# Silu in one instruction, b1 on sets of 32 partitions, mean terms by VectorE: a feed-forward block with cross-attention

## The chip, the cores and the metric

The kernel runs on one core of one Trainium2 chip. The metric is the device time of one execution in microseconds, the median of several runs.

## The reference

The input x has 32 tiles of 128 rows and 512 columns; ctx has the same shape, and a mask says for each of the 32 batches which of its 128 context rows count. With LN(x) = (x - mean) / sqrt(var + 1e-5):

```
scores = LN(x) @ ctx^T / sqrt(512), masked;  x = x + softmax(scores) @ ctx
y  = LN(x)
h  = silu(bitlinear(y, w1, b1))            # 512 -> 2048
h  = gelu(h, exact)
h  = layer_norm(h) * ln_g + ln_b           # over 2048
out = x + bitlinear(h, w2, b2)             # 2048 -> 512

bitlinear(x, w, b): xq = round(rms(x) * 127 / absmax) ...   # per row, 8 bits
                    wq = round(w / mean|w|) clipped to -1, 0, 1, times mean|w|
                    xq @ wq^T + b
```

## The kernel before

Everything is written by hand: five engine programs, each a list of calls in one fixed order, with semaphores between them. A tile t is one batch (128 rows). Each call below handles one tile, or two where it says (t, 2).

For a tile, TensorE sums the context's columns for two tiles at once (`column_sums`, L576 to 585, into the PSUM tensor `ba`). ScalarE multiplies these sums by the row means of x (`mean_term`, L1170, one instruction of 128 columns per tile), so that TensorE can work on x before it is normalised. `scores` (L564) adds a mask term (one row of `maskb` against ones, L569) and four fp32 products, in `ba` again, so the scores of a pair wait until its mean terms have been read out (`s_corr`). VectorE's `softmax` (L1902) centres them, ScalarE's `exp_scores` (L1164) takes exp, TensorE turns the probabilities and makes the readout (L587, L594), VectorE adds it to x (`add_readout`, L1916), GpSimd centres and rounds to q1 (L1555, L1569), and SyncE turns q1 by a transposing DMA.

The first product (`first_product`, L613) has two halves h. Each fills 1024 columns of `z_ps[h]` with eight matmuls of 512 columns (L623) and adds b1 with two more (L628), whose left side is `brows`, the turned factors of the tile, and whose right side is `rows1`, b1 in three bf16 parts crossed with three parts of the factor: 9 rows of 2048 columns. The factors are split by GpSimd (`split_factors`, L1576), turned by TensorE (L600), and copied by VectorE (`copy_factors`, L1950). ScalarE's `silu(t, h)` (L1192) reads one half, so that TensorE can refill the other half's PSUM as soon as one silu is done. Then come `gelu` (L1201) with its sum, the mean by GpSimd (`gelu_mean`, L1595), `variance` (L1207) on ScalarE, `rstd` on GpSimd (L1600), VectorE's three instructions of 2048 columns `gained`, `normed` and `norm_absmax` (L1961, L1973, L1982), ScalarE's `square_l` (L1218), GpSimd's rounding to q2 (L1612), a transposing DMA, the second product (`second_product`, L632) and `output` on VectorE (L2011).

Silu, gelu and exp need different function tables on ScalarE; where the order changes from one to another, the compiler puts an ACT_TABLE_LOAD. Squares, copies and scaling need none of their own. `warm` (L538) multiplies an idle tile, to keep TensorE working.

SyncE issues all DMAs in one written order. In the first 60 us it brings w1 and w2 (4 MB each, in quarters), gain and beta (1 MB each, broadcast to 128 partitions), and the first tiles of x, its transpose xT, ctx and its transpose ctxT (256 KB each). The weights are summed, scaled and rounded on three engines before the first product. The last tiles' rounding is split in halves between VectorE and ScalarE.

## Time and profile before

| | |
|---|---|
| median of 3 runs | 419.42 us (418.55 to 420.19) |
| the profiled execution | 418.72 us, span 416.8 us |
| ScalarE (ACT) busy | 381.7 us |
| TensorE (PE) busy | 380.0 us |
| VectorE (DVE) busy | 366.0 us |
| GpSimd (POOL) busy | 270.1 us |

Busy time is the union of an engine's instructions; a mean duration counts each alone, so neighbours that overlap add up to more than their share. The span is that of one execution in the hardware profile. PEld is TensorE's weight load, which overlaps its matmuls. PEclk, the clock granted to TensorE, is 1.00 at full speed.

### The profile page before, as it was taken

What the parts mean: (1) busy time and instruction counts of PE and PEld (TensorE: products, weight loads), DVE (VectorE), ACT (ScalarE), POOL (GpSimd) and SP (SyncE); (2) the same over time, 40 slices, a digit from 0 to 9 for tenths busy, and PEclk for the clock granted to TensorE, in tenths of its full rate; (3) what the DMA queues carried; (4) which work ended last, traced back from release to release, by engine and by line L of the source; (5) the groups of instructions that cost most, each with busy time, mean ns of one, the idle gap of its engine ahead of it and who ended that gap; (6) DMA issues with size and microseconds to landing.
All of it is one profiled execution on the core that took longest, in us unless ns stands there. A gap on an engine that the chain in (4) does not pass through costs nothing.

```text
span 416.8 us, 6814 instructions
## 1 busy us (share of the span) xinstructions
PE 380.0 (91%) x1878; PEld 202.8 (49%) x1878; DVE 366.0 (88%) x571; ACT 381.7 (92%) x517; POOL 270.1 (65%) x373
## 2 busy tenths in 40 slices
PE   3889888788999999999999999999999987899896
PEld 2576444444555544544555455554545432444342
DVE  5378589999999989999999999989998689999992
ACT  2597999999999999999999999999999999999960
POOL 6368588764787738664875569485368855477930
PEclk9999998999999999999999999999999996999999
DMA  7999991556665695658568765694754423083585
GB/s 290 412 366 320 393 289 39 176 131 143 196 172 119 177 225 158 157 164 197 150 168 239 201 171 147 201 218 102 187 133 94 91 63 63 2 201 102 90 213 128
DMA packets 108853, 73.87 MB, mean 177 GB/s; under 512 B 87048, under 2 KB 87056, under 8 KB 107536
## 3 DMA queue, kind: packets, MB, share of 16 engines
q1 hardware_dynamic: 108816, 73.43, 64.7%
q8 instruction: 16, 0.26, 0.3%
q14 instruction: 21, 0.17, 0.1%
HBM read 44.05 MB, written 8.39 MB: 126 GB/s over the span
## 4 chain that ended last, share of the span: by engine, by line
issue 23%; PE 22%; ACT 21%; DVE 19%; POOL 9%; DMA 4%; DVEq 0%; SPq 0%; POOLq 0%; ACTq 0%
ACT junk_v L1210 6%; DVE hid L1979 6%; PE z L623 6%; PE acc L648 5%; DVE hid L1970 5%; ACT hid L1205 4%; ACT hid L1199 4%; PE ba L573 3%; DMA xT<-in_xT_dram 3%; POOL hid L1616 3%; PE ba L584 2%; DVE am L1984 2%; PE z L628 2%; POOL rstd L1605 2%; PE bb L598 2%
## 5 line engine op out<-in xcount | busy, mean ns | idle before, releaser
L623 PE MATMUL z<-w1q,q1T 128*128 128x512 f16 x512 | 122.6, 383 | 3.9 <-ACT hid L1199 3.9
L648 PE MATMUL acc<-w2q,q2T 128*128 128x512 f16 x512 | 117.4, 379 | 1.2 <-DMA q2T<-hid 1.2
L1979 DVE SCALAR_TENSOR_TENSOR hid<-hid,rstd,beta 128x2048 f32<-128x2048 f32 x32 | 76.7, 2400 | 5.9 <-POOL rstd L1605 5.5
L623 PEld LDWEIGHTS z<-w1q,q1T 128*128 128x128 f16 x512 | 49.4, 98 | 65.1 <-ACT hid L1199 10.7
L1970 DVE SCALAR_TENSOR_TENSOR hid<-hid,nmu,gain 128x2048 f32<-128x2048 f32 x32 | 79.3, 2477 | 0.4 <-POOL nmu L1597 0.3
L648 PEld LDWEIGHTS acc<-w2q,q2T 128*128 128x128 f16 x512 | 49.8, 98 | 59.0 <-DMA q2T<-hid 2.0
L1984 DVE TENSOR_REDUCE am<-hid 128x1 f32<-128x2049 f32 x32 | 72.5, 2269 | 0.1
L1199 ACT ACTIVATE hid<-z,fac 128x1024 f32<-128x1024 f32 x64 | 70.7, 1118 | 0.8 <-PE z L628 0.5
L1221 ACT ACTIVATE junk_l<-hid 128x2050 bf16<-128x2050 f32 x32 | 61.1, 1910 | 3.7 <-DVE hid L1979 3.4
L1616 POOL TENSOR_SCALAR hid<-hid,kq 128x2048 f16<-128x2048 f32 x30 | 60.9, 2031 | 4.6 <-DVE kq L1991 3.0
L1210 ACT ACTIVATE junk_v<-hid,gsum 128x2048 bf16<-128x2048 f32 x32 | 63.7, 1990 | 0.1
L1205 ACT ACTIVATE hid<-hid 128x2048 f32<-128x2048 f32 x32 | 60.9, 1904 | 0.2
L628 PE MATMUL z<-rows,brows 128*128 128x512 bf16 x128 | 38.5, 383 | 1.4 <-DVE brows L1959 1.4
L584 PE MATMUL ba<-ctxT,neg 128*128 128x256 f32 x128 | 32.4, 398 | 6.5 <-DMA ctxT<-in_ctxT_dram 6.3
L573 PE MATMUL ba<-ctxT,xT 128*128 128x128 f32 x256 | 36.6, 287 | 1.9 <-DMA xT<-in_xT_dram 1.9
L1574 POOL TENSOR_SCALAR q<-xc,kq 128x512 f16<-128x512 f32 x32 | 33.8, 1056 | 4.9 <-DVE kq L1932 3.0
L598 PE MATMUL bb<-ctx,probT 128*128 128x512 f32 x64 | 34.2, 617 | 0.5 <-ACT probT L1181 0.5
L573 PEld LDWEIGHTS ba<-ctxT,xT 128*128 128x128 f32 x256 | 31.8, 195 | 4.7 <-issue 3.1
L1567 POOL TENSOR_TENSOR rho<-sq,c_neghalf 128x2 f32<-128x2 f32 (+1 forms) x17 | 14.7, 867 | 27.0 <-ACT junk_x L1189 27.0
L584 PEld LDWEIGHTS ba<-ctxT,neg 128*128 128x128 f32 x128 | 24.8, 199 | 12.7 <-issue 8.0
L1603 POOL TENSOR_SCALAR ve<-vsum 128x2 f32<-128x2 f32 (+1 forms) x18 | 9.9, 548 | 31.0 <-ACT junk_v L1210 30.6
L1920 DVE SCALAR_TENSOR_TENSOR xs<-bb,rsum,xs 128x512 f32<-128x512 f32 x32 | 23.8, 743 | 6.0 <-PE bb L598 5.9
(105 smaller groups left out, 569.4 us busy)
## 6 DMA issues: line engine op xcount, KB each, us to landing
ctxT<-in_ctxT_dram SPq DMA_DIRECT2D x32, 256.0 KB, 3.6
xs<-in_x_dram SPq DMA_DIRECT2D x32, 256.0 KB, 3.5
xT<-in_xT_dram SPq DMA_DIRECT2D x32, 256.0 KB, 3.7
ctx<-in_ctx_dram SPq DMA_DIRECT2D x32, 256.0 KB, 3.5
out_dram<-xs SPq DMA_DIRECT2D x32, 256.0 KB, 2.9
hid<-in_w1T_dram SPq DMA_DIRECT2D x4, 1024.0 KB, 9.4
hid<-in_w2T_dram SPq DMA_DIRECT2D x4, 1024.0 KB, 7.4
gain<-in_g_dram SPq DMA_DIRECT2D x1, 1024.0 KB, 10.5
```

The costliest lines, as they stand in the source:

```text
L573: mm = pe.matmul(score_ps, xT[:, t % XT, c, :], ctxT[:, t % CT, c, :], start=False, stop=(c == DC - 1))
L584: mm = pe.matmul(csum_ps, neg[:, :], ctxT[:, t % CT:t % CT + 2, c, :], start=(c == 0), stop=(c == DC - 1))
L623: pe.matmul(z_ps[h][:, c * CH:(c + 1) * CH], q1T[:, t % 4, k, :], w1q[:, k, f0:f0 + CH], start=(k == 0), stop=False)
L648: mm = pe.matmul(a, q2T[:, t % 2, c, :], w2q[:, c, :], start=False, stop=(c == FC - 1))
L1199: act.activation(hid[:, t % HR, half(h)], z_ps[h][:, :], ACT.Silu, scale=fac[:, t, 0:1]).then_inc(s_silu[h], 1)
L1205: act.activation(hh, hh, ACT.Gelu, accum_out=gsum[:, t:t + 1]).then_inc(s_gelu, 1)
L1210: act.activation(junk_v[:, :], hid[:, t % HR, 0:FF], ACT.Square, bias=gsum[:, t:t + 1], scale=-float(FF), accum_out=vsum[:, t:t + 1]).then ...
L1221: act.activation(junk_l[:, :], hid[:, row_of(t), 0:FF + 2], ACT.Square, scale=ROOT2, accum_out=ysum[:, t:t + 1]).then_inc(s_sq, 1)
L1616: pool.tensor_scalar(q2_of(t), hid[:, row_of(t), 0:FF], kq2[:, t:t + 1], UNIT, ALU.mult, ALU.mult).then_inc(s_q2, 1)
L1970: dve.scalar_tensor_tensor(out=hid[:, row_of(t), 0:FF], in0=hid[:, t % HR, 0:FF], scalar=nmu[:, t:t + 1], in1=gain[:, :], op0=ALU.add, op1 ...
L1979: dve.scalar_tensor_tensor(out=hh, in0=hh, scalar=rstd[:, t:t + 1], in1=beta[:, :], op0=ALU.mult, op1=ALU.add).then_inc(s_l, 1)
L1984: dve.tensor_reduce(am2[:, t:t + 1], hid[:, row_of(t), 0:FF + 1], AX_X, ALU.max, apply_absolute_value=True).then_inc(s_am2, 1)
```

## The change

- `z_ps` is one PSUM tensor of 2048 columns. `silu(t)` is one instruction over all of it; the first product of the next tile waits for the whole of it, and the signal that z is ready comes once per tile.
- The factors are repeated for four sets (bands) of 32 partitions. `rows1` is now 128 x 512: band c holds the rows for columns 512c to 512c+511. The four products with b1 come together at the end of the second half, each with 32 partitions of `brows` and of `rows1`, into four PSUM banks. `invert_factors` writes four copies, `split_factors` splits all of them, `copy_factors` copies 128 partitions instead of 18.
- The mean terms of two tiles are one VectorE instruction (`mean_terms`), and ScalarE has none. `gelu_mean` goes from GpSimd to VectorE.
- The mask is loaded by one DMA and turned into a bias once; `scores` picks its row by a column of the identity.
- `turn_factors` no longer waits for the output of an earlier tile by itself; that wait now stands in TensorE's order in front of the call.
- All five orders are written anew. Among other things, SyncE asks for x tiles 9 to 12 and beta ahead of gain (17.6 MB asked for up to and with gain before, 19.1 now) and for ctxT 8 and 9 later (16.6, now 20.1 MB); GpSimd rounds both of its w1 parts one behind the other; ScalarE's order has 51 changes of function table where it had 48; warm blocks go from 20 to 34, of which 29 stand ahead of the second product of tile 5; on VectorE 11 instead of 9 `x_stats` stand ahead of `gained(0)`, and `gelu_mean` of tiles 21, 22 and 23 ahead of `gained(21)`.

```diff
@@ first product, TensorE
-                wait(pe, s_silu[h], t)
-                pe.wait_ge(s_q1T[t % 4], landed(t, 4))
+                if h == 0:
+                    wait(pe, s_silu, t)
+                    pe.wait_ge(s_q1T[t % 4], landed(t, 4))
                 for k in range(DC):
-                    for c in range(2):
-                        f0 = h * HALF + c * CH
-                        pe.matmul(z_ps[h][:, c * CH:(c + 1) * CH], q1T[:, t % 4, k, :], w1q[:, k, f0:f0 + CH],
+                    for c in range(2 * h, 2 * h + 2):
+                        pe.matmul(z_ps[:, c * CH:(c + 1) * CH], q1T[:, t % 4, k, :], w1q[:, k, c * CH:(c + 1) * CH],
                                   start=(k == 0), stop=False)
-                pe.wait_ge(s_brow, t + 1)
-                for c in range(2):
-                    f0 = h * HALF + c * CH
-                    mm = pe.matmul(z_ps[h][:, c * CH:(c + 1) * CH], brows[:, t % 4, :], rows1[:, f0:f0 + CH],
-                                   start=False, stop=True)
-                mm.then_inc(s_z[h], 1)
+                if h == 1:
+
+                    pe.wait_ge(s_brow, t + 1)
+                    for c in range(BANDS):
+                        band = slice(c * BAND, (c + 1) * BAND)
+                        mm = pe.matmul(z_ps[:, c * CH:(c + 1) * CH], brows[band, t % 4, :], rows1[band, :],
+                                       start=False, stop=True)
+                    mm.then_inc(s_z, 1)
@@ silu, ScalarE
-                act.wait_ge(s_z[h], t + 1)
-                act.activation(hid[:, t % HR, half(h)], z_ps[h][:, :], ACT.Silu, scale=fac[:, t, 0:1]).then_inc(s_silu[h], 1)
+                act.wait_ge(s_z, t + 1)
+                act.activation(hid[:, t % HR, 0:FF], z_ps[:, :], ACT.Silu, scale=fac[:, t, 0:1]).then_inc(s_silu, 1)
@@ mean terms: ScalarE (gone) and VectorE (new)
-            def mean_term(t):
-
-                act.wait_ge(s_csp, t // 2 + 1)
-                act.wait_ge(s_mv1, t + 1)
-                wait(act, s_centred, t - CR + 1)
-                act.activation(corr[:, t % CR, :], csum_ps[:, t % 2 * P:(t % 2 + 1) * P], ACT.Identity,
-                               scale=mv1[:, t, 0:1]).then_inc(s_corr, 1)
+            def mean_terms(t):
+
+                dve.wait_ge(s_csp, t // 2 + 1)
+                dve.wait_ge(s_mv1, t + 2)
+                wait(dve, s_centred, t - CR + 2)
+                dve.tensor_tensor(corr[:, t % CR:t % CR + 2, :], csum_ps.rearrange("p (a m) -> p a m", a=2),
+                                  mv1[:, t:t + 2, 0:1].to_broadcast((P, 2, P)), ALU.mult).then_inc(s_corr, 2)
@@ mean of gelu: GpSimd (gone) and VectorE (new)
-            def gelu_mean(t):
-                pool.wait_ge(s_gelu, t + 1)
-                pool.tensor_scalar(nmu[:, t:t + 1], gsum[:, t:t + 1], -1.0 / FF, 0.0,
-                                   ALU.mult, ALU.add).then_inc(s_nmu, 1)
+            def gelu_mean(t):
+                dve.wait_ge(s_gelu, t + 1)
+                dve.tensor_scalar(nmu[:, t:t + 1], gsum[:, t:t + 1], -1.0 / FF, None, ALU.mult).then_inc(s_nmu, 1)
@@ factors, VectorE
-                dve.reciprocal(inv[:, of, :], fac[:, of, :]).then_inc(s_inv, n)
+                dve.reciprocal(inv[:, of, :, :], fac[:, of, :].unsqueeze(2).to_broadcast((P, n, BANDS, 2))).then_inc(s_inv, n)
@@ mask term, TensorE
-                pe.matmul(score_ps, ones_b[:, :], maskb[:, t // G % 2, t % G, :], start=True, stop=False)
+                pe.matmul(score_ps, ident_b[:, t:t + 1].to_broadcast((P, P)), maskb[:, :], start=True, stop=False)
```

## Rows read from the trace of the kernel before

**Rows 1.** The page: the span, and busy us (share of the span) xinstructions of each engine.

```profile
span 416.8 us, 6814 instructions
PE 380.0 (91%) x1878; PEld 202.8 (49%) x1878; DVE 366.0 (88%) x571; ACT 381.7 (92%) x517; POOL 270.1 (65%) x373
```

**Rows 2.** Busy us of each engine in four stretches; then clock, DMA share, GB/s.

```profile
0.00:40.00 40.00, 30.43 (x188) 22.60 (x189) 25.62 (x65) 23.04 (x46) 24.79 (x58) 1.00 0.95 344
40.00:57.30 17.30, 15.32 (x77) 8.35 (x75) 9.98 (x32) 17.19 (x27) 11.05 (x21) 1.00 1.08 365
57.30:400.00 342.70, 321.60 (x1560) 166.47 (x1558) 321.76 (x463) 338.32 (x443) 232.13 (x287) 0.99 0.60 149
400.00:416.80 16.80, 12.61 (x59) 5.37 (x57) 8.67 (x15) 3.15 (x3) 2.09 (x9) 0.98 0.62 164
```

**Rows 3.** Groups by line and form, ScalarE: busy us, mean ns | idle before.

```profile
L1199 ACT ACTIVATE hid<-z,fac 128x1024 f32<-128x1024 f32 x64 | 70.7, 1118 | 0.8 <-PE z L628 0.5
L1205 ACT ACTIVATE hid<-hid 128x2048 f32<-128x2048 f32 x32 | 60.9, 1904 | 0.2
L1199 ACT ACT_TABLE_LOAD x17 | 21.8, 1283 | 1.0 <-PE z L628 0.7
...
L1175 ACT ACTIVATE corr<-ba,mv 128x128 f32<-128x128 f32 x32 | 11.1, 365 | 4.1 <-PE ba L584 4.1
...
L1143 ACT ACTIVATE w2q<-hid 128x1024 f16<-128x1024 f32 x4 | 4.2, 1048 | 0.0
```

**Rows 4.** ScalarE's timeline from 180.8 to 185.7 us: start, us, what.

```profile
180.81 0.37 ACT L1175 ACTIVATE corr<-ba,mv 128x128 f32<-128x128 f32 x1
181.06 1.12 ACT L1199 ACTIVATE hid<-z,fac 128x1024 f32<-128x1024 f32 x1
182.06 0.29 ACT L1181 ACTIVATE probT<-bb 128x128 f32<-128x128 f32 x1
...
183.74 0.24 ACT L1189 ACTIVATION_READ_ACCUMULATOR junk_x<-xc 128x1 f32 x1
184.00 1.28 ACT L1167 ACT_TABLE_LOAD   x1
185.29 0.40 ACT L1167 ACTIVATE prob<-score,nbias 128x129 f32<-128x129 f32 x1
```

**Rows 5.** Groups by line and form, VectorE.

```profile
L1920 DVE SCALAR_TENSOR_TENSOR xs<-bb,rsum,xs 128x512 f32<-128x512 f32 x32 | 23.8, 743 | 6.0 <-PE bb L598 5.9
...
L1898 DVE BATCH_NORM_STATS2 st<-xs 128x6 f32<-128x512 f32 x32 | 22.1, 692 | 1.2 <-DMA xs<-in_x_dram 1.2
...
L1908 DVE CUSTOM_DVE_ANT_0 score<-corr,ba,nrs 128x128 f32<-128x128 f32 x32 | 11.0, 344 | 16.6 <-PE ba L573 14.1 <-POOL nrs L1553 2.1 <-issue 0.2
...
L1876 DVE TENSOR_SCALAR wfac<-wmean 128x1 f32<-128x1 f32 x2 | 0.3, 134 | 0.0
```

**Rows 6.** Groups by line and form, TensorE: the products with b1.

```profile
L628 PE MATMUL z<-rows,brows 128*128 128x512 bf16 x128 | 38.5, 383 | 1.4 <-DVE brows L1959 1.4
```

**Rows 7.** TensorE's timeline at 181 us: start, us, what.

```profile
181.25 0.59 PE L628 MATMUL z<-rows,brows 128*128 128x512 bf16 x2
181.68 0.22 PE L569 MATMUL ba<-maskb,ones_b 128*128 128x128 bf16 x1
```

**Rows 8.** The timeline of SyncE's queue: the issue of gain's load.

```profile
43.60 0.52 SPq L281 DMA_DIRECT2D gain<-in_g_dram  x1
```

**Rows 9.** The page's DMA issues: KB each, us from issue to landing.

```profile
gain<-in_g_dram SPq DMA_DIRECT2D x1, 1024.0 KB, 10.5
```

**Rows 10.** VectorE's timeline: its first instruction with gain.

```profile
57.27 2.35 DVE L1970 SCALAR_TENSOR_TENSOR hid<-hid,nmu,gain 128x2048 f32<-128x2048 f32 x1
```

**Rows 11.** TensorE's timeline: the column sums of tiles 8 and 9.

```profile
55.57 1.99 PE L584 MATMUL ba<-ctxT,neg 128*128 128x256 f32 x8 [0.21 <-DVE nbias L1908]
```

**Rows 12.** Waits of the whole span: engine line <- releaser: us in total, times, longest.

```profile
DVE hid L1979 <- POOL rstd L1605: 5.5, 8, 1.3
...
PEld ba L569 <- ACT corr L1175: 5.3, 5, 2.2
```

2046 lines of the change are left out of this document (974 added, 1072 removed).

## The prediction

> **What bounds the kernel now.** I read the page's busy times first. Three engines are nearly full over the 416.8 us of the profiled execution: ScalarE 381.7, TensorE 380.0, VectorE 366.0; GpSimd has 270.1 [rows 1]. An average over a start, a middle and a tail hides the limit, so I cut the span where VectorE begins its first 2048-column instruction (57.3 us) and where its last ones end (400). In the 342.7 us between, ScalarE is busy 338.32, which leaves it 4.4 us idle; TensorE has 321.60 (21.1 idle) and VectorE 321.76 (20.9 idle) [rows 2]. So the middle, four fifths of the time, goes at ScalarE's pace, about 11.7 us a tile. The start (0 to 57.3) is another matter: the DMA engines are full (shares 0.95 and 1.08) while 8 MB of weights and the first tiles come in [rows 2], and VectorE idles. In the last 16.8 us ScalarE is nearly done and VectorE works 8.67 us; what is left is the chain of the last tile. The reader should see that a microsecond taken from ScalarE is worth a microsecond only until the next engine is full, and that VectorE stands only 16.6 us behind in the middle.
>
> **ScalarE, what goes.** Silu was two instructions of 1024 columns, mean 1118 ns [rows 3]. One of 2048 is not in the trace. The step from 1024 to 2048 columns is taken from two forms of other functions, 1048 and 1904 ns [rows 3]: 0.856 us. So one whole silu is 1.118 + 0.856 = 1.974 us against 2.236, a gain of 0.26. But neighbours overlap: the silu that begins at 181.06 and lasts 1.12 is followed at 182.06 [rows 4], so of the fixed part only about 0.15 is time on the engine. With some 30 tiles in the middle that is 4.5 to 7.8 us, and I take 5, since the step from start to start is what fills an engine. The mean terms leave ScalarE: 365 ns each by duration [rows 3], 0.25 from start to start (180.81 to 181.06) [rows 4]; 24 of them lie in the middle, 6.0 to 8.8 us, and I take 7. The copy of b1 (9 rows of 2048 columns) becomes 128 rows of 512; it lies in the start, where the weights' arrival decides, so I give it nothing; it is worth about a microsecond if that cover is gone.
>
> **ScalarE, what is added.** A table load comes wherever the function changes between exp, silu and gelu; each is 1283 ns [rows 3]. Counting the changes in the written orders gives 48 before and 51 after, so 3 more: 3.85 us. The trace shows such a load between 184.00 and 185.28, directly behind the instruction that ended at 183.98 and directly ahead of the exp at 185.29 [rows 4]: nothing is lost around it. The Trainium skill, "ScalarE: Activation LUTs", section "What ACT_TABLE_LOAD costs", puts about 1380 ns of drain on top of the load's 1283 for every switch. By that rule the three added loads would be an estimated 8.0 us rather than 3.85, and the forecast 4 us later; the rows just read speak against it. Sum for ScalarE's middle: 338.3 - 5 - 7 + 3.9 = 330.2 us (bounds 325.6 and 331.7).
>
> **VectorE, what is added.** Mean terms: 16 instructions over 2 x 128 columns of PSUM, about 12 in the middle. Nearest rows are the softmax step with 128 columns from PSUM, 344 ns, and the readout's addition with 512, 743 ns [rows 5]; on the line between them 256 columns cost 0.48. Less an overlap of the same kind as on ScalarE, 0.4 to 0.48: 4.8 to 5.8 us; the lower end could be 12 x 0.28, but a tensor operand that reads two tiles at once gives no reason for less. The mean of gelu moves over from GpSimd, one value per partition: 134 ns by the nearest row [rows 5], and less where it overlaps: 30 x 0.08 to 30 x 0.13, 2.4 to 4. The reciprocal over 16 instead of 4 values and the copy of factor rows from 128 instead of 18 partitions cost nothing that shows (lanes work side by side). Two more x_stats stand ahead of the first gained than before (11 against 9 in the two orders): -2 x about 0.8, from 692 ns [rows 5]. Sum: 321.8 + 5.3 + 3.0 - 1.6 = 328.5 us (bounds 327.4 and 330).
>
> So after the change ScalarE (330) and VectorE (328.5) carry the same load in the middle. That is the core of the forecast: about 8 us leave the bounding engine, and the next one rises by 7 to meet it.
>
> **TensorE.** The four products with b1 last 383 ns each [rows 6], but two are through in 0.59 us and the next instruction begins 0.43 behind the first (181.25, 181.68) [rows 7]: a step of 0.216, so 0.86 us of a tile's time. If the four run at once on four sets of 32 partitions, 0.22 is left, a saving of 0.64 x 30 = 19 us; if they run one behind the other, nothing. TensorE has 21 us idle in the middle already [rows 2] and waits for others, so I give either case nothing in the sum. With z in one piece, the next tile's first product must wait for the whole silu (1.97) where it waited for half; the written order puts readouts, scores or second products there, and ScalarE has two squares of 2048 and two of 512 columns between most pairs of silus, some 5 us by the 1904 ns of such a length [rows 3], more than a first product (16 x 0.216 = 3.5) needs. So nothing, and up to 1 us a pair if the filler is late. Of the 34 warm blocks 29 stand in the first part, ahead of the second product of tile 5, where TensorE waits anyway.
>
> **GpSimd** loses 32 means and 7 mask instructions and gets four times wider splits of the factors, from 4 to 16 values and from 12 to 48; it is busy 65% and pays nothing.
>
> **The start.** I add up the bytes in the written order of SyncE's queue, up to and with gain: 17.6 MB before, 19.1 after (more x tiles, and beta ahead of gain). Gain was issued at 43.60 [rows 8] and landed 10.5 us later [rows 9], at 54.1, and the first gained began at 57.27 [rows 10], 3.2 later. At the 365 GB/s of that stretch [rows 2], 1.5 MB more are 4.3 us: landing at 58.4, 1.1 later than the instruction began. w1's columns are rounded earlier by the new GpSimd order, but that can't bring the first gained ahead of its operand. So +1.1 (0 if the queue runs fuller, 3 if SyncE's waits for q1 hold it). Context tiles 8 and 9 move back as well, from 16.6 to 20.1 MB, so to about 61; their column sums began at 55.57 [rows 11] and stand ahead of the first product of tile 3 on TensorE. That is late by up to 3 us, and ScalarE has the squares and gelus of tiles 0 to 2 to cover it; without that cover it is the same 3 us.
>
> **The sum.** VectorE: 58.4 (start) + 328.5 (work) + idle in the middle + 16.8 (tail, left as it is). That is 403.7 + idle. The bounding engine of before idles 4.4 us; VectorE, which had to wait for it, 20.9. With both equally loaded I take 8, above the first, since each now waits for the other: the largest of VectorE's waits for another engine's result, 5.5 us for rstd, comes through GpSimd from ScalarE's variance [rows 12], and gets shorter as ScalarE gets ahead. Span 411.7. The profiled execution ran 418.72 for a span of 416.8, so +1.9: 413.6, against its own 418.72. The median of the runs, 419.42, stands 0.7 above that execution: 414.3 is predicted.
>
> **The rivals.** (A) VectorE has taken ScalarE's place fully and the idle hardly shrinks: idle 12 to 13, which gives 403.7 + 12.5 + 2.6 = 418.8, no change. For it: the new VectorE order puts up to three means of gelu (21, 22, 23) ahead of gained(21), so that VectorE waits for a later gelu than it needs. Against it: ScalarE gains 8 us. (B) The products with b1 don't run side by side, or TensorE pays for each change between whole and banded products. A matmul lasts 383 ns and steps 216 [rows 6, 7], so a change that waits for the last one to end is priced at the difference, 0.17; two such per tile are 10 us in the middle. Serial and with that, TensorE has 321.6 + 10 = 331.6, a third engine at the same load, with idle of about 13: 419. The Trainium skill, "TensorEngine Tiling (Array Packing)", section "Key Properties", says that a change of tiling mode drains the engine; no row of before shows one. With the four at once and that price, TensorE is at 312 and harmless. (C) Slower: the mean terms now queue on VectorE behind its instructions of 2.35 us [rows 10], with the scores waiting for them on TensorE and everything behind these in order. Before, TensorE's weight loads for the scores waited 5.3 us in all for them [rows 12]. TensorE's idle of 21 plus the 19 saved are some 2.7 us per pair of tiles; the wait decides once it is over that. One such instruction in front stays below, two in front (4.7) are 2.0 over, at 15 pairs up to 30 us. With a quarter of the pairs: 414.3 + 8 = 422 to 423. Against it: in the new order a column sum stands at least 3.5 us of other products ahead of its scores. (D) Better: start unchanged, idle 4.4, lower prices: 57.3 + 327.4 + 16.8 + 4.4 + 2.6 = 408.5.
>
> **How the numbers follow.** Forecast (idle 6 to 11) 0.42; D 0.22; A 0.12; B 0.07; C 0.17. Faster by over 0.5% means under 417.3: forecast and D, 0.64. Within 0.5%, about what a measurement here can tell from no change: A and B, 0.19. Slower than 421.5: C, 0.17. The range reaches from 407 (D with silu at its best) to 423 (the near side of C).
>
> **What the next profile would show.** Right: silu x32 at 1.97 us; 51 loads; mean terms 0.4 to 0.5 on VectorE; VectorE busy 373 to 378 and ScalarE 366 to 371; VectorE idle in the middle under 11; first gained at 58 to 59; TensorE busy below 370 and the four band products within 0.6 us. Wrong: scores waiting for the mean terms by more than 10 us in all (C); a gained longer than the 2.35 us of before; band products stepping at 216 ns (B); a start that is later by more than 3 us.

## The result, and the profile after

The changed kernel takes 425.44 us (median of 4 runs, 422.52 to 426.14) against 418.99 for the kernel before in the same series: ratio 1.013, interval 1.0106 to 1.0154. It is slower, by 1.3%. The prediction was 414.3 us, with a range of 407 to 423, and faster as the likeliest sign. The profiled execution took 422.52 us for a span of 420.7, 3.9 more than the 416.8 of [rows 1]. It is the shortest of the four; the other three took 425.25 to 426.14 us, spans of 423.5 to 424.3. So what follows accounts for these 3.9 us, and some 2.5 of the 6.45 by which the medians differ are not in the trace.

The page of the changed kernel, the span and the engines' busy time:

```profile
span 420.7 us, 6729 instructions
PE 375.8 (89%) x1943; PEld 199.8 (47%) x1962; DVE 366.7 (87%) x619; ACT 373.4 (89%) x456; POOL 281.1 (67%) x333
```

Against [rows 1] ScalarE lost 8.3 us of work, TensorE 4.2, VectorE gained 0.7 and GpSimd 11.0. No engine got fuller in share except GpSimd, and the time still rose, so the time has gone into waits. To see where, I cut both traces at two events of ScalarE that exist in both: its first silu, and the gelu of tile 26. First the kernel before (columns as in rows 2):

```profile
0.00:39.44 39.44, 29.87 (x186) 22.34 (x187) 25.06 (x64) 22.48 (x46) 24.23 (x58) 1.00 0.95 343
39.44:343.02 303.58, 287.33 (x1398) 151.91 (x1396) 277.31 (x440) 300.33 (x413) 203.90 (x263) 0.99 0.65 171
343.02:416.80 73.78, 62.77 (x296) 28.55 (x296) 63.66 (x68) 58.89 (x60) 41.93 (x54) 0.95 0.49 113
```

and the kernel after:

```profile
0.00:44.90 44.90, 38.01 (x225) 26.54 (x226) 24.66 (x64) 19.39 (x38) 21.17 (x58) 0.92 1.00 349
44.90:343.23 298.33, 278.71 (x1440) 147.00 (x1453) 278.00 (x483) 293.10 (x363) 218.18 (x232) 1.00 0.64 165
343.23:420.70 77.47, 59.12 (x279) 26.25 (x283) 64.06 (x74) 60.90 (x56) 41.76 (x44) 0.96 0.49 116
```

Three stretches, three answers. The middle is 5.25 us shorter, and ScalarE's own work in it 7.2 us shorter; this is what the change was costed for. The first silu comes 5.5 us later. From gelu(26) to the end it takes 3.7 us longer. The sum is +3.9, the whole difference of the spans. With the old start and the old end the new middle would have given a span of 411.55. That this is close to the forecast's 411.7 is chance: the forecast had the start 1.1 later and its own middle, cut at other places, 6.2 shorter.

The operations themselves, groups by line and form of the kernel after (ScalarE, VectorE, TensorE):

```profile
L1120 ACT ACTIVATE hid<-z,fac 128x2048 f32<-128x2048 f32 x32 | 62.8, 1962 | 0.7 <-PE z L622 0.5
L1120 ACT ACT_TABLE_LOAD x19 | 24.4, 1283 | 2.6 <-PE z L622 2.3
L1125 ACT ACT_TABLE_LOAD x18 | 23.1, 1283 | 0.3
L1096 ACT ACT_TABLE_LOAD x14 | 18.0, 1283 | 0.9 <-PEq L2366 0.7
...
L1825 DVE SCALAR_TENSOR_TENSOR hid<-hid,nmu,gain 128x2048 f32<-128x2048 f32 x32 | 75.8, 2375 | 5.9 <-ACT junk_v L1130 5.8
L1761 DVE TENSOR_TENSOR corr<-ba,mv 128x256 f32<-128x256 f32 x16 | 6.6, 412 | 0.5 <-DVE mv L1744 0.4
...
L615 PE MATMUL z<-w1q,q1T 128*128 128x512 f16 x512 | 120.3, 385 | 14.4 <-ACT hid L1120 14.4
L622 PE MATMUL z<-rows,brows 32*128 32x512 bf16 x128 | 12.6, 385 | 0.0
```

The whole silu lasts 1.962 us (costed at 1.974), the mean terms of two tiles 0.412 (costed at 0.40 to 0.48), and there are 51 table loads, as costed. The products with b1 fell from 38.5 us of TensorE's time [rows 6] to 12.6. What they cost now is seen in TensorE's timeline (start, us, what):

```profile
50.48 0.40 PE L622 MATMUL z<-rows,brows 32*128 32x512 bf16 x4
50.80 0.33 PE L585 MATMUL bb<-ident,prob 128*128 128x128 f32 x1
```

Four products are through in 0.40 us, and the next instruction begins 0.32 behind the first, where four steps of 0.216 would have been 0.86 [rows 7]. They do run at once. TensorE as a whole did not fall below 370 us as forecast (375.8), since 14 warm blocks were added. Beside it stands a row that the forecast had priced at nothing, and up to 1 us a pair: TensorE's first product (L615) now waits 14.4 us for silu, 3.9 before.

VectorE, on whose load the predicted sum was built, from its first instruction with gain to the last instructions (the cut lies as far behind the last normed as in rows 2):

```profile
60.95:402.80 341.85, 309.98 (x1573) 158.89 (x1589) 320.58 (x503) 334.82 (x397) 245.54 (x250) 0.99 0.59 144
```

Of 341.85 us VectorE is busy 320.58 and idle 21.3. Before it was busy 321.76 and idle 20.9 [rows 2]. In the same stretch ScalarE is busy 334.82 and idle 7.0: it is still the engine with the least idle time. What makes up VectorE's idle time has changed. The wait for rstd fell from 5.5 to 4.0 us, but `gained`, which may only write over the tile when ScalarE's `variance` has read it, now waits 5.8 us for that (the row of L1825 above); before, `gained` waited 0.4 us in all.

### The profile page after: what moved, and what is told of

The parts are those of the page before. It is cut to its first block, busy times and chain, and to the rows that moved or that the text cites. A ratio compares the mean times of both kernels' runs of the same rounds, so it can differ in the third digit from the quotient of the medians.

```text
span 420.7 us, 6729 instructions
## 1 busy us (share of the span) xinstructions
PE 375.8 (89%) x1943; PEld 199.8 (47%) x1962; DVE 366.7 (87%) x619; ACT 373.4 (89%) x456; POOL 281.1 (67%) x333
## 4 chain that ended last, share of the span: by engine, by line
ACT 36%; issue 22%; PE 21%; DVE 14%; DMA 4%; SPq 1%; POOL 1%; ACTq 0%; DVEq 0%; POOLq 0%
ACT hid L1120 8%; PE z L615 7%; ACT junk_v L1130 6%; ACT hid L1125 6%; PE acc L642 6%; ACT junk_l L1141 4%; DVE hid L1825 4%; ACT L1125 3%; ACT L1120 3%; PE ba L566 3%; DVE hid L1834 2%; DMA xs<-in_x_dram 2%; DVE am L1839 2%; ACT L1096 2%; PE bb L591 2%
## 5 line engine op out<-in xcount | busy, mean ns | idle before, releaser
L615 PE MATMUL z<-w1q,q1T 128*128 128x512 f16 x512 | 120.3, 385 | 14.4 <-ACT hid L1120 14.4
L615 PEld LDWEIGHTS z<-w1q,q1T 128*128 128x128 f16 x512 | 49.4, 99 | 75.9 <-ACT hid L1120 19.9
L1825 DVE SCALAR_TENSOR_TENSOR hid<-hid,nmu,gain 128x2048 f32<-128x2048 f32 x32 | 75.8, 2375 | 5.9 <-ACT junk_v L1130 5.8
L1499 POOL TENSOR_SCALAR hid<-hid,kq 128x2048 f16<-128x2048 f32 x30 | 65.1, 2173 | 10.5 <-ACT junk_l L1141 5.6
L1120 ACT ACTIVATE hid<-z,fac 128x2048 f32<-128x2048 f32 x32 | 62.8, 1962 | 0.7 <-PE z L622 0.5
L1448 POOL TENSOR_SCALAR xc<-xs,sum 128x512 f32<-128x512 f32 x32 | 33.8, 1055 | 11.9 <-DVE xs L1772 11.4
L1486 POOL TENSOR_SCALAR ve<-vsum 128x2 f32<-128x2 f32 (+1 forms) x18 | 17.6, 980 | 30.1 <-ACT junk_v L1130 29.8
L1461 POOL TENSOR_SCALAR q<-xc,kq 128x512 f16<-128x512 f32 x32 | 28.6, 896 | 9.6 <-DVE kq L1784 8.4
L534 PE MATMUL z<-idle 128*128 128x256 bf16 x204 | 27.6, 285 | 1.6 <-POOL idle L1384 1.1
L1869 DVE SCALAR_TENSOR_TENSOR xs<-acc,fac,xs 128x512 f32<-128x512 f32 x32 | 23.5, 738 | 6.3 <-PE acc L642 6.1
L1742 DVE BATCH_NORM_STATS2 st<-xs 128x6 f32<-128x512 f32 x32 | 21.6, 676 | 6.7 <-DMA xs<-in_x_dram 6.7
```

The lines of the kernel that those rows point to most:

```text
L615: pe.matmul(z_ps[:, c * CH:(c + 1) * CH], q1T[:, t % 4, k, :], w1q[:, k, c * CH:(c + 1) * CH], start=(k == 0), stop=False)
L1120: act.activation(hid[:, t % HR, 0:FF], z_ps[:, :], ACT.Silu, scale=fac[:, t, 0:1]).then_inc(s_silu, 1)
L1499: pool.tensor_scalar(q2_of(t), hid[:, row_of(t), 0:FF], kq2[:, t:t + 1], UNIT, ALU.mult, ALU.mult).then_inc(s_q2, 1)
L1825: dve.scalar_tensor_tensor(out=hid[:, row_of(t), 0:FF], in0=hid[:, t % HR, 0:FF], scalar=nmu[:, t:t + 1], in1=gain[:, :], op0=ALU.add, op1 ...
```

## The experiments

A run is named here by its kernel; "before" and "after" are the two kernels of the case. The table gives, for the profiled execution of each, four times read from ScalarE's timeline and the span, and beside them the ratio of the timed runs to before. The times are of one execution each, and executions of one kernel differ by up to 6 us (p6_nosilu: 442.71 to 448.65), so small differences in these columns prove nothing by themselves.

| kernel | silu(0) | gelu(2) | gelu(26) | gelu(31) | span | ratio (interval) |
|---|---|---|---|---|---|---|
| before | 39.44 | 69.99 | 343.02 | 392.44 | 416.8 | 1 |
| after | 44.90 | 74.78 | 343.23 | 394.50 | 420.7 | 1.013 (1.0106 to 1.0154) |
| p1_silu | 43.77 | 80.01 | 397.92 | 451.60 | 476.0 | 1.1397 (1.1358 to 1.1435) |
| p4_ops | 44.40 | 77.90 | 393.07 | 446.24 | 471.0 | 1.1282 (1.1248 to 1.1316) |
| p3_mean | 44.94 | 74.71 | 367.63 | 417.04 | 441.4 | 1.054 (1.0502 to 1.0578) |
| p6_nosilu | 42.43 | 72.28 | 370.63 | 421.65 | 446.8 | 1.0651 (1.0589 to 1.0713) |
| p7_mean_placed | 39.81 | 69.60 | 346.23 | 395.67 | 420.0 | 1.0092 (1.0065 to 1.0119) |
| a1_halves | 42.75 | 72.94 | 344.65 | 397.19 | 424.7 | 1.017 (1.0134 to 1.0205) |
| e1_warm | 42.42 | 74.04 | 342.50 | 393.78 | 420.1 | 1.0111 (1.0059 to 1.0162) |
| e5_warm_moved | 44.73 | 74.43 | 342.94 | 394.21 | 420.4 | 1.0127 (1.0068 to 1.0186) |
| e2_warm_stats | 42.27 | 76.75 | 346.05 | 398.53 | 425.9 | 1.0165 (1.0114 to 1.0216) |
| h1_oldstart | 40.26 | 76.34 | 345.62 | 398.18 | 427.3 | 1.019 (1.0164 to 1.0216) |
| h3_oldstart_sp | 41.00 | 72.39 | 340.86 | 393.45 | 422.4 | 1.0076 (1.0042 to 1.0109) |
| e3_tail | 42.12 | 74.90 | 343.37 | 396.91 | 427.1 | 1.0236 (1.019 to 1.0282) |
| e6_end | 43.59 | 74.71 | 343.24 | 395.63 | 424.2 | 1.0144 (1.0119 to 1.0169) |
| e8_end_warm | 42.95 | 75.78 | 344.28 | 396.79 | 423.7 | 1.0104 (1.0043 to 1.0165) |
| e9_end2 | 41.81 | 73.14 | 341.63 | 394.15 | 419.8 | 1.0078 (1.0051 to 1.0106) |
| e7_start_end | 41.98 | 75.48 | 343.99 | 396.22 | 421.9 | 1.0081 (1.0053 to 1.0109) |
| h2_oldstart_end | 40.62 | 75.40 | 343.93 | 396.47 | 423.4 | 1.0147 (1.0115 to 1.0178) |
| h4_both | 40.14 | 71.85 | 340.30 | 392.85 | 418.5 | 1.0034 (1.0015 to 1.0053) |

One reading of the table first: from gelu(2) to gelu(26) it takes 273.03 us in before, and 268.4 to 268.6 in after and in ten kernels that share its middle (269.3 in e2_warm_stats and h1_oldstart). So the middle's gain of 3.7 to 4.6 us is there every time.

### What each part costs on the old orders

**p1_silu**: the kernel before, with only z in one piece and silu whole.

```diff
-act.wait_ge(s_z[h], t + 1)
-act.activation(hid[:, t % HR, half(h)], z_ps[h][:, :], ACT.Silu, scale=fac[:, t, 0:1]).then_inc(s_silu[h], 1)
+act.wait_ge(s_z[0], t + 1)
+act.wait_ge(s_z[1], t + 1)
+act.activation(hid[:, t % HR, 0:FF], z_ps[:, :], ACT.Silu, scale=fac[:, t, 0:1]).then_inc(s_silu, 1)
```

> The kernel before, with one part of the change alone: z in one piece, silu in one instruction of 2048 columns in the place of the second half's, all orders as before. Theory S: ScalarE bounds, the saving is 0.15 us a tile, 32 x 0.15 = 4.8 us, less what TensorE's first products lose by waiting for the whole: ratio 0.989 to 0.995. Rival W: on these orders, ScalarE waits for z that comes late because TensorE may not refill before the whole silu is read; each pair loses a microsecond or more, ratio 1.01 to 1.04.

477.58 us. The part that saves ScalarE 3.9 us of work costs 58 us on the old orders. Its waits (engine line <- releaser: us in total, times, longest):

```profile
PE z L623 <- ACT hid L1200: 43.6, 17, 4.7
ACT hid L1200 <- PE z L628: 38.1, 14, 5.2
```

TensorE waits for silu, and then silu for TensorE, in turn: with one z, and the calls in this order, little is left to work on while the other side is busy. In before the same first wait was 3.9 us.

**p4_ops**: every operation of the changed kernel on the orders of before; calls that moved to another engine stand at the nearest place.

```diff
-silu(24, 0)
-mean_term(30)
-mean_term(31)
-silu(24, 1)
+silu(24)
...
 x_stats(25)
+mean_terms(24)
...
+gelu_mean(24)
 gained(24)
```

> All the operations of the changed kernel (whole silu, b1's four products on sets of 32 partitions, mean terms of two tiles and gelu's mean on VectorE, mask in one) on the orders of the kernel before, the moved calls put in at the nearest place. Theory O (the new orders lose): with 48 table loads, the old start and the old end, it runs 6 to 8 us below the changed kernel, ratio 0.995 to 1.0. Rival Q (the operations themselves lose): mean terms behind VectorE's long instructions hold TensorE, and the ratio is 1.013 or more on whatever order.

472.87 us, 5 less than p1_silu. So of the changed kernel's two sides, the operations lose 54 us on the old orders and the new orders win 47 of them back. The orders aren't a side matter: without them the new operations are ruinous.

**p3_mean** and **p7_mean_placed**: before, with the mean terms alone moved to VectorE. They differ only in where some of the 16 instructions stand: close behind the pair's statistics in p3_mean, and in p7_mean_placed where, in the trace of before, the pair's column sums had just ended. One of the moves, from p3_mean to p7_mean_placed:

```diff
 x_stats(25)
-mean_terms(24)
 norm_absmax(15)
...
 normed(16)
+mean_terms(24)
 x_stats(26)
```

> The kernel before with one part alone: mean terms of two tiles by one VectorE instruction, each placed in VectorE's old order between the pair's statistics and its first softmax and never between two 2048-column instructions; silu stays in halves. Theory M (this part pays alone, since ScalarE sets the pace): ScalarE busy 381.7 less 32 times 0.3 = about 371, time 412 to 416, ratio 0.985 to 0.993. Theory Q (the terms queue behind VectorE's 2.35 us instructions and scores wait for them, the prediction's rival C): ScalarE busy falls the same, but TensorE's wait on the mean terms grows by over 10 us in all, ratio 1.00 to 1.02.

442.18 us: the first form costs 23 us. TensorE's wait for the terms did not grow as theory Q had it; VectorE was the one that stood, waiting for column sums that TensorE's order had not reached, with all that is queued behind it. VectorE's and ScalarE's timelines (start, us, what, and the idle time before it):

```profile
252.14 0.42 DVE L1912 TENSOR_TENSOR corr<-ba,mv 128x256 f32<-128x256 f32 x1 [6.22 <-PE ba L584]
252.48 2.28 DVE L1987 TENSOR_REDUCE am<-hid 128x1 f32<-128x2049 f32 x1
...
263.02 1.91 ACT L1213 ACTIVATE junk_l<-hid 128x2050 bf16<-128x2050 f32 x1 [6.54 <-DVE hid L1982]
```

6.2 us idle on VectorE, 10 us later 6.5 us idle on ScalarE.

> The kernel before with the mean terms on VectorE alone, as in the run that took 442.2 us, but each of the 16 instructions placed where, in the trace of before, the pair's column sums had just left TensorE (that run placed them up to 6.2 us too early, and VectorE stood still in its order behind them). Theory P (the place is the price): the waits of 6.2 and 5.4 us go, ScalarE's wait for VectorE's normed tile falls from 14.7 us to under 5, and ScalarE keeps its 11 us: 410 to 416 us, ratio 0.98 to 0.993. Rival (these small steps on VectorE are late wherever they stand, since 2.35 us instructions lie ahead of them, and the start loses the same 5 us): 420 to 430 us, ratio over 1.003.

422.79 us: the place was worth 19 us, as theory P said. But P's second half fell. ScalarE lost the work (in the middle 294.93 us busy against 300.33) and the middle took 306.42 us against 303.58. It idles 11.5 us there instead of 3.3, the largest share for VectorE's normed tiles (5.0 us over the run). ScalarE's work fell by 7.0 us over the whole run (381.7 to 374.7), 0.22 a tile and not the 11 us of the mean terms' durations; put in small pieces on the next engine, it gave nothing on the old orders. silu(0) is 0.4 us later than in before (39.81), so mean terms on VectorE need not delay the start.

**p6_nosilu**: all operations except the one-piece z, on the old orders, mean terms placed as in p3_mean.

```diff
+if h == 0:
+    for c in range(2):
+        band = slice(c * BAND, (c + 1) * BAND)
+        mm = pe.matmul(z_ps[:, c * CH:(c + 1) * CH], brows[band, t % 4, :], rows1[band, :], start=False, stop=True)
+    mm.then_inc(s_za, 1)
```

> Every operation of the changed kernel except silu in one piece, on the orders of before: mean terms and the small sum on VectorE, b1's products on 32-partition bands (two at once behind each half), the mask as one table; z is released and made ready per half as before. Beside the same with silu whole (472.9 us) it differs only in the one-piece z. Theory H (the one-piece z is the whole loss of the old orders): within 1% of the run with the mean terms alone, ratio 0.98 to 1.00, TensorE's wait for silu back to 3 to 6 us. Rival (bands, mask or the small sum on VectorE cost something by themselves): over 1.01.

447.41 us, 1% over p3_mean, and 25 us under p4_ops, which has the one-piece z besides. So the one-piece z costs 25 us with all else equal here (58 when it is added to before alone), and bands, mask and the small sum on VectorE about 5 together, the difference to p3_mean (one comparison, not taken apart further). Why the one-piece z costs twice as much on before alone was not tested.

### Halves on the new orders

**a1_halves**: after, its orders kept, with silu again in two instructions.

```diff
-silu(t)
+silu(t, 0)
+silu(t, 1)
```

TensorE refills columns 0 to 1023 of z behind the first of the two, and for 23 of the tiles the first half is made ready by itself; tile 0 is not among them.

> The changed kernel, its orders kept, with silu again in two instructions of 1024 columns next to each other; TensorE refills the first half of z after the first instruction, and for 23 of the tiles the first half is made ready alone. Theory S (handshake): the new orders still pay for the one-piece z at the start and at the end; ScalarE busy +5 us, but silu(0) starts 0.5 to 1 us earlier and TensorE's 14.4 us wait for silu falls under 6; time 420 to 425, ratio 1.002 to 1.013, equal to or faster than the changed kernel. Theory R (ScalarE's time is all that counts in the middle): +4 to +5 us, ratio 1.022 to 1.025.

426.33 us, 0.9 more than after; the two ratios' intervals overlap. TensorE's wait for silu fell from 14.4 us to 3.0, as S had it, and brought nothing: from gelu(2) to gelu(26) it takes 271.7 us instead of 268.5, and from silu(0) to gelu(26) ScalarE has 297.4 us of work instead of 293.1. So on orders made for it the one-piece z is worth its work in the middle, and the 14.4 us of waiting cost nothing there. silu(0) comes 2.15 us earlier than in after, but not by the halves: it still waited for all four products with b1. TensorE's first product began at 35.69 instead of 37.36, at a full clock. The ratio of 1.017 lies between what S and R gave. Of the end this run says nothing: a first product there waited 4.8 us for the transposing DMA of its q1.

### The start

The first product of tile 0 is on TensorE's timeline, and silu(0) follows it. Before, from the product's beginning to the two products with b1 that make the first half of z ready, and the same in e9_end2, whose start is that of after call for call:

```profile
35.74 1.89 PE L623 MATMUL z<-w1q,q1T 128*128 128x512 f16 x8
37.47 0.59 PE L628 MATMUL z<-rows,brows 128*128 128x512 bf16 x2
```

```profile
34.71 1.89 PE L615 MATMUL z<-w1q,q1T 128*128 128x512 f16 x8
40.02 0.40 PE L622 MATMUL z<-rows,brows 32*128 32x512 bf16 x4
```

| kernel | z of tile 0 | first product | silu(0) | between |
|---|---|---|---|---|
| before | halves | 35.74 | 39.44 | 3.70 |
| h4_both (old start order) | halves | 36.55 | 40.14 | 3.59 |
| p1_silu (old order) | one piece | 36.16 | 43.77 | 7.61 |
| after | one piece | 37.36 | 44.90 | 7.54 |
| e3_tail (start as after) | one piece | 35.10 | 42.12 | 7.02 |
| e6_end (start as after) | one piece | 36.98 | 43.59 | 6.61 |
| e8_end_warm (start as after) | one piece | 36.55 | 42.95 | 6.40 |
| e9_end2 (start as after) | one piece | 34.71 | 41.81 | 7.10 |

With z of tile 0 in halves silu(0) comes 3.6 to 3.7 us behind the first product in all eight kernels that have it so, and with the whole of z to wait for 6.4 to 7.6 us in the other twelve. So the handshake costs 2.7 us or more at the start, in every execution; in e3_tail and e9_end2 the first product even began earlier than before, and silu(0) was still 2.7 and 2.4 us late. The rest of the 5.5 us of after is of its own execution, and differs from one to the next.

In the trace of after TensorE idles 2.19 us in front of the fifth tile's scores, waiting for VectorE's mean terms; and then its granted clock falls. VectorE's and TensorE's timelines:

```profile
29.05 0.69 DVE L1742 BATCH_NORM_STATS2 st<-xs 128x6 f32<-128x512 f32 x1 [1.53 <-DMA xs<-in_x_dram]
29.88 2.33 DVE L1725 TENSOR_SCALAR w1q<-hid,wscale 128x2048 f16<-128x2048 f32 x1
32.27 0.40 DVE L1761 TENSOR_TENSOR corr<-ba,mv 128x256 f32<-128x256 f32 x1
...
32.72 0.23 PE L562 MATMUL ba<-maskb,ident_b 128*128 128x128 bf16 x1 [2.19 <-DVE corr L1761]
32.82 2.03 PE L566 MATMUL ba<-ctxT,xT 128*128 128x128 f32 x8
37.36 3.03 PE L615 MATMUL z<-w1q,q1T 128*128 128x512 f16 x8
```

Read upwards: the scores wait for mean terms, these stand behind a 2.33 us rounding step of w1, and that stands behind the statistics of tile 5, whose x came 1.53 us late. The granted clock of 30 to 40 us is 0.66, between its two levels of 2.4 and 1.2 GHz. The eight products for scores take 2.03 us; the same eight take 1.11 at full clock (57.07 us), and the half first product 3.03 against 1.89. This is rival C's mechanism, with one 2.33 us instruction in front, in one place instead of a quarter of the pairs: from 100 to 340 us the scores waited only 0.2 us for mean terms. The same wait is in e6_end (2.20 us), but in e3_tail and e9_end2, with the same calls up to there, it is 0.25 us, x was not late, and the clock stays 1.00. So this chain is something that an execution can meet, and not the price of the order.

**e1_warm**: idle matmuls in that gap.

```diff
 readout(2)
+warm(34)
+warm(35)
+warm(36)
 pe.wait_ge(s_corr, 6)
 scores(4)
```

> The changed kernel with three warm blocks (18 matmuls of 256 columns on the idle tile, about 2 us) added on TensorE between the readout of tile 2 and the scores of tile 4. Theory Z (TensorE's clock): in the changed kernel TensorE stands idle for 2.2 us ahead of those scores, then the granted clock is at the lower of its two levels from about 32 to 40 us, and the scores (2.0 instead of 1.1 us), the readout (2.1 for 1.0) and the first half of the first product (3.0 for 1.9) take some 3 us more on the way to the first silu. With the gap filled the first silu begins at about 42 instead of 44.9 us and the whole comes 3 us earlier, a ratio to the kernel before near 1.006. Rival Y (the start is hidden): VectorE or the DMAs decide when the pipeline is full, the first silu comes earlier but the end stays, 1.013.

The clock stays 1.00 from 20 to 45 us and silu(0) comes 2.5 us earlier than in the trace of after. That this is the blocks' doing is not shown: e3_tail and e9_end2 have it at 42.12 and 41.81 without them. gelu(2) is 0.7 earlier, and the time 423.88 (1.0111), its interval over that of after. silu(2) waits 1.9 us for a first product that stands behind four more warm blocks.

**e5_warm_moved**: e1_warm without these four.

```diff
-warm(14)
-warm(15)
 readout(5)
-warm(16)
 scores(7)
-warm(17)
 first_product(2, 0)
```

> The changed kernel with three blocks of idle matmuls between the third readout and the fifth tile's scores (they keep the clock up, as in the first experiment), and without the four blocks 14 to 17 that stood ahead of the third tile's first product. In the first experiment silu(2) waited 1.94 us for that product, behind 3.3 us of idle matmuls. Theory N (those blocks took back what the clock gave): gelu(2) starts at 72.0 to 72.8 instead of 74.0, time 421 to 422.5, ratio 1.004 to 1.008. Rival (the pair after it is held by VectorE or a load, or the clock falls again without the blocks): gelu(2) at 74 or later, ratio 1.011 or more.

silu(2) no longer waits for z, but in this execution the clock had already fallen to 0.54 from 15 to 20 us, silu(0) came at 44.73, and the ratio is 1.0127. Undecided on its own: taking idle matmuls out at one place while the clock falls at another.

**e2_warm_stats**: two warm blocks, and the rounding step ahead of tile 5's statistics.

```diff
 readout(2)
+warm(34)
+warm(35)
...
 softmax(3)
-x_stats(5)
 round_w1(1)
+x_stats(5)
```

> The changed kernel with, at the start, two blocks of idle matmuls after the third readout and VectorE's rounding step of w1 ahead of tile 5's statistics, which waited 1.5 us for tile 5's load. Theory N2 (the wait for the load shifts the mean terms of the third pair and with them silu(0)): silu(0) at 41.0 to 42.0 instead of 44.9, and since the blocks 14 to 17 are still there, gelu(2) only at about 73.5 to 74: ratio 1.008 to 1.012. Rival (another input is late): silu(0) at 42.4 or later, no gain on the first experiment.

silu(0) at 42.27, no better than e1_warm, in whose execution x(5) had not been late (0.04 us), so a late x(5) is not what remains. gelu(2) came at 76.75, with a granted clock of 0.89 from 45 to 75 us. A miss: 1.0165.

**h1_oldstart**: each engine works off the order of before up to about 53 us, with silu of tiles 0 and 1 in halves and mean terms placed as in p7_mean_placed; then the rest of the new order, without warm blocks 14 to 17.

```diff
 weight_total(1)
-pe.wait_ge(s_corr, 8)
-scores(6)
-pe.wait_ge(s_wmean[1], 1)
-turn_factors(2)
 pe.wait_ge(s_turn, 6)
 readout(4)
+pe.wait_ge(s_wmean[1], 1)
+turn_factors(2)
+pe.wait_ge(s_corr, 8)
+scores(6)
 turn_factors(3)
 pe.wait_ge(s_silu, 2)
-warm(14)
-warm(15)
 readout(5)
...
```

Shown is the seam in TensorE's order (behind turn_factors(2)); on ScalarE it lies behind gelu(1), on VectorE behind x_stats(8), on GpSimd behind centre_x1(5), and on SyncE behind load_beta. Calls already made are left out of the rest.

> All operations of the changed kernel; each engine first works off the order of before up to about 53 us (ScalarE up to the gelu of tile 1, with mean terms placed as in the run of 422.8 us and silu of tiles 0 and 1 in halves), and then the rest of the new order, with silu in one piece and without the idle blocks 14 to 17. Theory L (what was lost at the start is the new start order with its one-piece z, and the middle of the changed kernel is good by itself): silu(0) at 39.5 to 40.5, gelu(2) at 70 to 71.5 instead of 74.8, span 416 to 418, ratio 0.995 to 1.002. Rival F (what is late at 75 us is VectorE's and GpSimd's backlog, which comes back in another place): gelu(2) earlier, but gelu(8) at 142 or later, ratio 1.008 or more.

silu(0) is 4.6 us earlier than in after, 3.59 us behind a first product that began at 36.67. Then everything waited for one transpose. SyncE's queue and TensorE:

```profile
56.18 1.20 SPq L257 DMA_TRANSPOSE q1T<-q  x1
...
66.08 2.29 PE L621 MATMUL z<-w1q,q1T 128*128 128x512 f16 x5 [5.95 <-DMA q1T<-q]
```

In before tile 3's transpose was issued at 45.41; here the seam had put it behind four x loads and, among others, two ctxT loads that wait for free buffers.

**h3_oldstart_sp**: that one line moved.

```diff
 load_beta()
+transpose_q1(3)
 load_x(10)
...
 load_xT(8)
-transpose_q1(3)
```

> The old start on the new middle once more, with one line moved in SyncE's queue: the transpose of tile 3's q1 stands where it stood in before, right behind the load of beta, instead of behind four x loads, the gain's followers and four ctxT loads. In the first try silu(0) was 4.6 us earlier than in the changed kernel, but tile 3's first product waited 5.95 us for this transpose (issued at 56.2 instead of 45.4) and gelu(2) came at 76.3. Theory L: gelu(2) at 69.5 to 71.5, span 415.5 to 418, ratio 0.994 to 1.002. Rival F (backlog of the other engines): gelu(2) early, gelu(8) at 141.5 or later, ratio 1.006 or more.

gelu(2) 72.39, 4 us earlier than in h1_oldstart, 2.4 earlier than in after, and it keeps this to gelu(26) (340.86 against 343.23). 423.57 us, ratio 1.0076. Theory L is right in kind: something was lost at the start, and what is won back there is kept through the middle. But it is half of the 4.8 us by which gelu(2) was late, and in this execution the end, unchanged, takes 81.5 us from gelu(26) instead of 77.5, more than was won. Old order and halves came together in the h kernels; by the table above silu(0) is earlier by the halves, since the first product is not (37.41).

### The end

Between gelu(26) and the end ScalarE has 2.0 us more to do (60.90 against 58.89): two of the three extra table loads lie there, since the new order goes from silu to gelu and back for each of the last tiles. And VectorE asks for the small sum of tile 31 ahead of the row maximum of tile 30, so it waits for gelu(31), and outputs, scales and TensorE's last products are late in turn.

**e3_tail**: after, with ScalarE's order from silu(28) as in before, two loads fewer.

```diff
 silu(28)
-gelu(28)
 square_l(24)
 square_l(25)
-variance(28)
 silu(29)
+gelu(28)
 gelu(29)
+variance(28)
...
```

> The changed kernel with the end of ScalarE's order (from silu of tile 28 on) laid as in the kernel before: silu 28, silu 29, gelu 28, gelu 29 instead of silu, gelu, silu, gelu; 49 function-table loads instead of 51, two fewer than in the changed kernel, both in the end. Theory T: ScalarE bounds up to the last silu, so the two loads (2 x 1.28 us) are worth 2.6 us and the end is 2 to 3.7 us earlier, ratio 1.004 to 1.008. Rival: VectorE's 2048-column instructions set the last 70 us, the loads are hidden, ratio 1.013.

428.66 us, 4.8 slower than e1_warm of the same series. silu(29) waits 1.8 us for z and silu(30) 3.6. So in this order the two loads fewer are paid for with longer waits for the one z: two silus can't follow each other closely. Theory T fell.

**e6_end**: VectorE's end reordered, three warm blocks left out.

```diff
-warm(31)
-warm(32)
-warm(33)
 second_product(28, 0)
...
-gelu_mean(31)
 norm_absmax(30)
 output(27)
 copy_factors(34)
+gelu_mean(31)
 gained(31)
...
+q2_scale(31, 1)
 output(28)
 out_scale(31, 1)
-q2_scale(31, 1)
```

> The changed kernel with its last 30 us rearranged only: on VectorE the row maximum of tile 30 goes ahead of tile 31's small sum (which waited 0.83 us for tile 31's gelu with the row maximum behind it), tile 31's scale goes ahead of tile 28's output, and TensorE's three blocks of idle matmuls ahead of the last four second products are left out. In the trace of after these products began at 401.63, 4.3 us later than in before, and then ran almost without a gap. Theory E (the order at the end costs over 2 us of the 3.7): span 1.8 to 3 us shorter than 420.7, ratio 1.005 to 1.009. Rival (the end hangs on the two extra table loads and on gelu(31), 2.1 us late): under 1 us, ratio 1.011 or more.

1.0144, a miss. The last products began at 399.33 instead of 401.63, but then TensorE idled 2.26 and 1.48 us, the granted clock fell to 0.50 (410 to 415 us), and eight products took 3.62 us instead of 1.89. It was also slow earlier, where nothing had been changed. The same two stretches of after and of e6_end:

```profile
370.00:375.00 5.00, 3.90 (x20) 1.41 (x19) 4.89 (x7) 4.97 (x6) 3.30 (x6) 0.92 1.11 208
375.00:380.00 5.00, 4.95 (x24) 2.24 (x24) 4.00 (x3) 4.97 (x5) 1.34 (x2) 1.00 0.02 4
```

```profile
370.00:375.00 5.00, 3.53 (x10) 1.08 (x9) 4.89 (x7) 4.97 (x6) 3.31 (x6) 0.50 1.12 208
375.00:380.00 5.00, 4.95 (x25) 2.08 (x25) 4.00 (x3) 3.87 (x5) 1.36 (x2) 0.97 0.02 5
```

At a clock of 0.50 instead of 0.92, tile 30's first product is 1.1 us late and ScalarE idles 1.1 us (4.97 busy against 3.87). gelu(30) comes 42.55 us behind gelu(26) in after, e1_warm and e5_warm_moved, and 43.5 to 43.9 in a1_halves, e2_warm_stats, e6_end, e7_start_end, e8_end_warm, e9_end2 and the four h kernels. That is in kernels with and without a changed end, so I can't put it down to an order.

**e8_end_warm**: the same VectorE order, the warm blocks between the last products (the same three are gone ahead of them).

```diff
 second_product(29, 1)
+warm(31)
+warm(32)
+warm(33)
 pe.wait_ge(s_o, 29)
 turn_factors(36)
+warm(37)
+warm(38)
```

> The rearranged end once more, with the three blocks of idle matmuls put where TensorE stood still in the last try (between the second product of tile 29 and the factors' transposes for tile 30, and two more behind the first of these) instead of left out. In that try the last products began 2.3 us earlier, but after an idle time of 2.3 and 1.5 us the granted clock was 0.50, and 8 products of tile 30 took 3.6 us instead of 1.9. Theory K (order plus clock make the end): span 2 to 3 us shorter than 420.7, ratio 1.004 to 1.009. Rival (the end hangs on gelu(31), which is 2.1 us late by the two extra table loads): ratio 1.011 or more.

1.0104. Now the idle time ahead of the products did it, TensorE's timeline:

```profile
400.27 0.23 PE L603 MATMUL acc<-ident_b,bcols 128*128 128x128 bf16 x1 [1.81 <-DVE xs L1871]
400.49 0.51 PE L636 MATMUL acc<-rows,brows 128*128 128x512 bf16 x1
400.80 5.21 PE L642 MATMUL acc<-w2q,q2T 128*128 128x512 f16 x16
```

After 1.81 us idle the first 16 products take 5.21 us instead of 3.62.

**e9_end2**: warm blocks in both gaps.

```diff
 turn_factors(34)
+warm(31)
+warm(32)
 pe.wait_ge(s_o, 28)
 turn_factors(35)
-warm(31)
-warm(32)
-warm(33)
...
 second_product(29, 1)
+warm(33)
 pe.wait_ge(s_o, 29)
 turn_factors(36)
+warm(37)
```

> The changed kernel with the rearranged end and idle blocks in the two places in which TensorE stood still in the last tries: two while it waits for the output of tile 27 (ahead of the last products, not behind the transpose), one ahead of and one behind the factors' transposes for tile 30. In the last try the second scale of tile 31 came 12.6 us after gelu(31) began (14.2 in the changed kernel), and that was lost when 16 products after a 1.8 us idle time took 5.2 us instead of 3.6. Theory K: from gelu(31) to the end 24 to 24.8 us instead of 26.2, ratio 1.006 to 1.011. Rival: 26 us or more again.

The 16 products are back at 3.6 us, and 422.24 us (1.0078) is the best of the kernels that keep the new start. From gelu(31) to the end it takes 25.65 us, 0.55 less than after, not the 1.4 to 2.2 that theory K had. Of the end's 3.7 us this accounts for about half a microsecond; ScalarE has 2.0 us more work there with the two table loads, which stay, though no run shows what they cost at the end; the rest is not settled.

### Together

**e7_start_end**: e2_warm_stats without warm blocks 14 to 17, with e6_end's end.

```diff
+warm(34)
+warm(35)
...
-warm(14)
-warm(15)
...
-x_stats(5)
 round_w1(1)
+x_stats(5)
...
-gelu_mean(31)
 norm_absmax(30)
...
```

> The changed kernel with the rearranged start (two idle blocks and the rounding step ahead of tile 5's statistics), without the idle blocks 14 to 17 ahead of the third first product, and with the rearranged end of the run beside it. Theory (start and end add up): silu(0) at 41 to 42, gelu(2) at 71.5 to 72.5, end 2 us shorter: span 415 to 417, time 417 to 419, ratio 0.995 to 1.0. Rival (each later stage takes the gain back): ratio over 1.004.

1.0081: a little better than after (the intervals just overlap), without reaching before. The clock was 0.89 from 45 to 75 us and gelu(2) came at 75.48.

**h2_oldstart_end** is h1_oldstart with the end of e8_end_warm; **h4_both** is h3_oldstart_sp with the end of e9_end2.

```diff
+transpose_q1(3)
 load_x(10)
...
-gelu_mean(31)
 norm_absmax(30)
 output(27)
 copy_factors(34)
+gelu_mean(31)
 gained(31)
```

> The start of before and the rearranged end in one kernel, middle as changed. By theories K and L together: span 413.5 to 416, ratio 0.988 to 0.997, faster than before. By the rivals together: ratio 1.005 or more.

1.0147, with the late transpose of h1_oldstart in it.

> Both together: the old start with the moved transpose, the new middle, and the end as in the run beside it. By L and K: span 413.5 to 416, ratio 0.990 to 0.998. By the rivals: 1.004 or more.

420.30 us, median of 12 runs, ratio 1.0034 (1.0015 to 1.0053): the best of all variants, and still 0.3% behind before. Its three stretches:

```profile
0.00:40.14 40.14, 31.40 (x185) 22.80 (x186) 24.17 (x66) 19.50 (x40) 21.25 (x56) 1.00 0.92 334
40.14:340.30 300.16, 278.77 (x1427) 145.91 (x1440) 278.16 (x481) 293.53 (x363) 217.20 (x235) 1.00 0.66 171
340.30:418.50 78.20, 60.70 (x285) 26.83 (x289) 64.33 (x74) 60.90 (x56) 41.01 (x44) 0.95 0.48 115
```

Start +0.7 against before, middle -3.4, end +4.4. The changed kernel loses 6.45 us in the medians and this one 0.9. Against after, silu(0) is 4.8 us earlier, the middle 1.8 longer (part of the start's gain is given back up to gelu(2)) and the end 0.7 longer. What is left against before is the end, which takes the whole of the middle's gain.

## Why the prediction was wrong

**The step that failed** is VectorE's idle time in the middle, taken at 8 us and found at 21.3. Term by term, for the forecast's own stretches of the span:

| term | forecast | found | difference |
|---|---|---|---|
| start, up to the first gained | 58.4 | 60.95 | +2.6 |
| VectorE's work | 328.5 | 320.6 | -7.9 |
| VectorE's idle time | 8 | 21.3 | +13.3 |
| tail | 16.8 | 17.9 | +1.1 |
| span | 411.7 | 420.7 | +9.0 |

The median stands another 2.1 us away, since it lies 4.7 above the profiled span and not 2.6.

**The sum was made on an engine that is not the bound.** The work term was 8 us too high: mean terms and small sums came as costed, but gained and normed take 5.4 us less in all, which no row had suggested; the rest is spread over small changes. Since ScalarE still set the pace, that gave nothing, and idle time took its place. The idea that waits shrink when two engines get equal loads had no case here: the loads were not equal (334.8 and 320.6), the wait for rstd got shorter as forecast (5.5 to 4.0 us), and a wait of gained for ScalarE's variance (5.8 us) came in its place. In p7_mean_placed too ScalarE lost work and only idled more.

**ScalarE's gain: right in size, and smaller where it counts.** The silu was within 1% of its estimate, and by a1_halves, which differs in it alone, the whole silus save 5.0 us of ScalarE's work (378.4 against 373.4), the 5 that were taken. The loads' number and length are exact. The mean terms were taken at 7 us for the 24 of the middle, and p7_mean_placed shows 7.0 for all 32, so some 5.3. Together, 5.0 + 7.0 - 3.85 is 8.2, and ScalarE lost 8.3 in the whole run, where 366 to 371 us had been forecast against 373.4. Between silu(0) and gelu(26) its work fell by 7.2 us and the time by 5.25. In the forecast's stretch it came to 334.8 instead of 330.2, since 5.4 us of work that had been done ahead of the first gained now lie behind it (40.2 us [rows 2] against 34.8). The forecast's middle is only 0.85 us shorter than before (341.85 against 342.70): it contains 2.6 us of what the end lost.

The load still costs its 1.28 us and no more: in after one runs from 53.14 to 54.42, right behind silu's data, and gelu begins at 54.43. So what the Trainium skill, "ScalarE: Activation LUTs", section "What ACT_TABLE_LOAD costs", says of some 1380 ns on top isn't seen in this kernel, before or after.

**TensorE at nothing: right for the middle on the new orders, wrong for the start.** The bands work as hoped (0.32 us a tile, rival B is out; the drain that "TensorEngine Tiling (Array Packing)", section "Key Properties" of the Trainium skill, tells of is at most the 0.10 us by which 0.32 exceeds one product's 0.22). The one-piece z was costed at "nothing, and up to 1 us a pair". On the old orders it is 58 us alone (p1_silu). The new orders hide it in the middle (a1_halves, where 11 us less of waiting bring no time), but not at the start, where silu(0) now waits for all four bands instead of half the columns: 6.4 us or more behind the first product against 3.7. At the end it ties the order of silu and gelu to more table loads, which cost less than the waits without them (e3_tail).

**The start: +1.1 predicted, +3.7 found** for the first gained (60.95), and 5.5 for silu(0). The prediction followed gain through SyncE's queue. Gain was issued at 51.1 and landed 7.0 later, at 58.1, 0.3 from the predicted 58.4; but gained(0) was not waiting for it. In the new order it stands behind the small sums of tiles 0 and 1. VectorE waited 1.37 us for the gelu of the first, up to 56.47, and then worked almost without a gap up to gained(0). Neither the wait for the whole of z nor the order of VectorE's start was priced, nor the chain that this execution met (late x(5), rounding step, mean terms, scores, low clock).

**The tail "left as it is": wrong by 3.7 us** if counted from gelu(26); in the last stretch behind VectorE's cut it is 17.9 us against the 16.8 taken over. The diff showed that silu and gelu alternate there, and the table loads were counted, but put in the middle.

**The rivals.** C ended on the right side, with 422 to 423 for a median of 425.44, and for the wrong reason: from 100 to 340 us the scores waited 0.2 us for mean terms. Its mechanism acted once, at 32 us, and not in every execution. A had the idle time staying high (12 to 13), nearer to the 21.3 than the forecast, but its time (418.8) rested on VectorE being the bound, which it was not. The range of 407 to 423 missed the median by 2.4 us, since start and tail had no upper bounds of their own beyond 3 us for one of them.

## What to carry to other kernels

When a change removes one of two buffers between two engines, price it by the handshake: with one z, each side's whole turn is a wait for the other unless the order puts as much independent work between, and at the start there is none to put. Build a sum on the engine that sets the pace; the idle time of another one is what is left over, and not a term of its own. A gain in the steady middle is worth what start and end leave of it; cut the span at events both kernels have, and give each stretch its own term and its own range. Before a chain of waits in one trace is called the cause, look whether another execution of the same calls has it. And in a kernel with written orders, a small step moved to another engine has its price in its place: the same 16 instructions cost 23 us or 3.

## What the hardware showed besides

TensorE's granted clock was part of many differences here. Behind idle times of 1.8 to 2.3 us it stood at 0.66 (after, 30 to 40 us), 0.50 (e6_end, 410 to 415) and 0.83 (e8_end_warm, 400 to 410), and the same start differed between executions: e1_warm and e5_warm_moved have the same orders up to their first silu, yet one had it at 42.42 and the other at 44.73, and with the start of after it came at 41.81 to 44.90. With idle matmuls in the gap the clock stayed at 1.00 (e1_warm, 20 to 45 us; it did so in e9_end2 without them), and they delayed whatever stood behind them (e1_warm's silu(2), 1.9 us).

The same instructions of VectorE and GpSimd took other times. VectorE's gained went from 2477 to 2375 ns on average and GpSimd's rounding of q2 from 2031 to 2173 and its centring from 818 to 1055, while its rounding of q1 went from 1056 to 896. GpSimd is busy 281.1 us instead of 270.1 although its means and seven mask steps are gone. The traces settle what these means hide. A centring or rounding step on GpSimd takes about 0.70 us (rounding of q2: 1.97) if neither gained nor normed is running when it begins, in all but two of 168 cases of the two traces, and 2.28 to 2.83 us (q2: 3.70 to 4.04) if one is, in all 20. The other way, 14 of the 64 gained and normed took over 2.45 us before and 3 after (up to 3.47), and in 12 of the 14 and all 3 such a step of GpSimd was already running. So each holds up the other, the one that began second waits, and a mean duration tells how often they met. That they met less often on VectorE's side is why gained and normed became cheaper.
